# Attention with a routed FFN on one core: where ScalarE copies the transposed inverse sums out of PSUM

## The reference

```python
s1 = jnp.einsum('bhtd,bhsd->bhts', q1, k1) * scale + mask
s2 = jnp.einsum('bhtd,bhsd->bhts', q2, k2) * scale + mask
a1 = jax.nn.softmax(s1, axis=-1)
a2 = jax.nn.softmax(s2, axis=-1)
diff = a1 - lam * a2
out = jnp.einsum('bhts,bhsd->bhtd', diff, v)
```

## Time and profile before

| | |
|---|---|
| runs, device time | 2269.70, 2272.86, 2258.52 us (median 2269.7) |
| the profiled execution | 2265.93 us, span of the core 2264.1 us |
| TensorE busy | 1808.6 us (80% of the span) |
| VectorE busy | 1458.3 us (64%) |
| ScalarE busy | 1129.6 us (50%) |
| GpSimd busy | 614.6 us (27%) |
| granted TensorE clock, mean | 0.878 of full speed |
| attention | about 58 to 1520 us of the span |
| L763, the copy that is moved | 128 instructions |

### The profile page before, as it was taken

One profiled execution on the slowest core, in us unless ns is written; L12 is line 12 of the kernel. 1 busy time (PEld: TensorE's weight loads), 2 busy tenths in 40 slices (PEclk: granted clock), 3 DMA queues, 4 the chain that ended last, 5 costly groups with the idle time before them and its releaser, 6 DMA issues. The chain is left out here.

```text
span 2264.1 us, 37174 instructions
## 1 busy us (share of the span) xinstructions
PE 1808.6 (80%) x9826; PEld 1336.3 (59%) x9827; DVE 1458.3 (64%) x3278; ACT 1129.6 (50%) x3263; POOL 614.6 (27%) x504
## 2 busy tenths in 40 slices
PE   3678898898889879879888888967099999999700
PEld 3455555656655755655655564544099999999600
DVE  2588867878788788787787878751333333333366
ACT  1466756667566575676667766661122222222133
POOL 2222312412231242241232223110542222200165
PEclk7788898899889889799989989988599999999855
DMA  7855534545454463453545455320543333223288
GB/s 262 282 139 152 145 99 140 178 112 149 134 166 120 126 200 114 124 174 103 159 151 147 129 152 168 75 75 19 181 146 112 112 114 120 74 83 98 73 269 269
DMA packets 142837, 319.51 MB, mean 141 GB/s; under 512 B 16704, under 2 KB 19264, under 8 KB 140512
## 3 DMA queue, kind: packets, MB, share of 16 engines
q1 hardware_dynamic: 113280, 241.84, 37.8%
q0 software_dynamic: 14432, 48.64, 6.4%
q10 hardware_dynamic: 14976, 27.27, 3.2%
HBM read 215.97 MB, written 109.05 MB: 144 GB/s over the span
## 5 line engine op out<-in xcount | busy, mean ns | idle before, releaser
L735 ACT ACTIVATE expd<-S,neg_max 128x128 f32<-128x128 f32 (+3 forms) x1024 | 530.7, 534 | 158.7 <-DVE neg_max L878 156.2
L878 DVE TENSOR_REDUCE neg_max<-S 128x2 f32<-128x768 f32 (+3 forms) x384 | 399.7, 1041 | 278.9 <-PE S L598 277.5
L909 DVE SCALAR_TENSOR_TENSOR mixed<-expd,rho 128x384 f32<-128x384 f32 (+3 forms) x512 | 337.2, 678 | 0.3 <-issue 0.3
L747 ACT ACTIVATE probsT<-PTp 128x512 f32<-128x512 f32 (+2 forms) x384 | 203.7, 531 | 254.0 <-PE PTp L609 251.3
L490 POOL TENSOR_TENSOR swapped<-swapped,rope_t 128x512 f32<-128x512 f32 x80 | 103.3, 1291 | 767.2 <-DVE swapped L864 767.2
L594 PE MATMUL S<-kT,qT 128*128 128x256 f32 (+2 forms) x1024 | 285.8, 382 | 27.4 <-DMA qT<-parts_rows 13.4
L609 PE MATMUL PTp<-ident,mixed 128*128 128x128 f32 x1280 | 221.3, 290 | 102.3 <-DVE mixed L909 99.7
L644 PE MATMUL tail<-wo,ctxT 128*128 128x512 f32 x512 | 252.9, 622 | 24.9 <-ACT ctxT L779 22.2
L594 PEld LDWEIGHTS S<-kT,qT 128*128 128x128 f32 x1024 | 165.7, 199 | 127.5 <-issue 82.4
L1311 ACT ACTIVATE xT_hi<-xTp 128x512 fp32r<-128x512 f32 x72 | 43.1, 599 | 359.2 <-DVE yo L1487 348.9
L609 PEld LDWEIGHTS PTp<-ident,mixed 128*128 128x128 f32 x1280 | 145.3, 148 | 126.6 <-DVE mixed L909 123.5
(11 more groups left out here) (206 smaller groups left out, 3631.1 us busy)
## 6 DMA issues: line engine op xcount, KB each, us to landing
qT<-parts_rows SPq DMA_DIRECT2D x256, 256.0 KB, 4.6
parts_rows<-parts SPq DMA_DIRECT2D x160, 256.0 KB, 2.0
wqk<-wqk_split SPq DMA_DIRECT2D x75, 512.0 KB, 5.2
xin<-expert_in_rows SPq DMA_DIRECT2D x72, 256.0 KB, 2.9
expert_out_rows<-yo ACTq DMA_DIRECT2D x72, 256.0 KB, 3.2
kT<-parts_rows SPq DMA_DIRECT2D x64, 256.0 KB, 4.3
x<-in_x SPq DMA_DIRECT2D x8, 1024.0 KB, 7.8
x_rows<-x SPq DMA_DIRECT2D x8, 1024.0 KB, 7.0
```

The source lines that it names most:

```text
L735: ex = nc.scalar.activation(expd[s % 3][:, k * slot:k * slot + w], S[s % 2][:, k * slot:k * slot + w], ACT.Exp, bias=neg_max[s % 3][:, k:k ...
L747: nc.scalar.activation(probsT[i % 2][:, 0:i + 1, half:half + n, pair, :].rearrange("p j a q -> p a j q"), PTp[:, 0:w].rearrange("p (a j q) ...
L878: nc.vector.tensor_reduce(neg_max[s % 3][:, 0:k], v, AX, ALU.max, negate=True).then_inc(max_ready, 1)
L909: ins = nc.vector.scalar_tensor_tensor(out=mixed[sl % 3][:, a * 256:a * 256 + w], in0=e2, scalar=rr[:, i, h:h + 1], in1=e1, op0=ALU.mult, ...
```

## The change

In ScalarE's walk through the steps, the call of `take_scale` stands behind `exps` instead of in front of `take_probsT`. The condition is the same, so each of the 128 copies stays in its step. The short code behind the last batch (`end`), which has two of the copies, is as it was.

```diff
             def body(b, par, first, last):
                 for s, kv, u in steps(b, first, last):
-                    if (s - LAG_V - 1) % NU in LAST_OF and lagged(b, s, LAG_V + 1, first):
-                        take_scale(tile_no(b, s, LAG_V + 1))
                     if lagged(b, s, LAG_T, first):
                         take_probsT(*lagged(b, s, LAG_T, first), tile_no(b, s, LAG_T))
                     exps(s, u)
+                    if (s - LAG_V - 1) % NU in LAST_OF and lagged(b, s, LAG_V + 1, first):
+                        take_scale(tile_no(b, s, LAG_V + 1))
                     if (s - 2) % NU in LAST_OF and lagged(b, s, 2, first):
                         widen(*lagged(b, s, 2, first), tile_no(b, s, 2))
```

## The result

The changed kernel takes 2284.6 us (median of 12 runs, 2278.4 to 2292.2) against 2269.6 us (12 runs, 2258.5 to 2272.9). The ratio is 1.007, with a 95% interval of 1.0053 to 1.0088: slower by 12 to 20 us. Forecast were +33 us and 2302. The direction is right, the time is inside the stated range, and the size is off by a factor of two. The time is just under the forecast's own 2285 to 2320 and inside the 2270 to 2290 of the first rival. The profiled execution has a span of 2280.0 us (before 2264.1), and all of the difference but about 3 us lies between the first maximum of attention and the last.

A forecast was written before the change was run, and what follows sets the result against it. Each batch was taken as bound by a loop between engines, chiefly TensorE and VectorE. Removal 0 plus mean 4.1 us added per batch made 33 us over eight; from median 2270 that gave 2303, stated 2302, range 2268 to 2338.

The forecast's parts named there:

- the first rival: "The waits are absorbed": slack at the 16 places and TensorE catching up leave half or less, 2270 to 2290 us; chance 0.28.
- What goes away: Copy no longer in front of `probsT` on ScalarE: charged at nothing, since ScalarE would wait for the same transposes; bound 49 us.
- What is added: VectorE's L917 waits for the later copy, delaying the next maximum: 6.3 us in one batch, 5.2 in the next, 46 over eight.
- three kinds of places: Of 16 per batch: seven where VectorE is late itself, four where the maximum waits for scores, five where new waits count.
- (a): Step 8 of the second kv head: maximum 1.3 us later, 0.8 us after slack.
- (b): Step 0: maximum 1.8 us later, 0.7 in the next batch; after slack 1.4 and 0.3 us.
- (d): Step 8 of the fourth kv head: maximum 1.2 us later, no slack taken off.
- (e): Step 12 of the batch: maximum 1.2 us later but covered by ScalarE's `ctxT` work; only the copy counts, 0.4 us.
- (c): Step 4: maximum 0.8 us later, no slack taken off.
- How much reaches the end: Share of VectorE's new waits that delays TensorE: 4.7 us in one batch, 3.6 in the next, 33 us over eight.
- Faster: ScalarE no longer idles in front of the copy, 0.384 us gained per copy on the path, down to 2217 us; chance 0.06.
- The clock rival: Added waits lower TensorE's granted clock from 0.89 to 0.86 in a batch, 45 us in all, 2344 us; chance 0.08.

The follow-up runs named there:

- e4: Kernel before with only the copies of step 6 (tile 0) moved behind the exponentials: ratio 1.001, +2 us.
- e11: Changed kernel with VectorE's product (L917) of tiles 1 and 2 behind the maximum of steps 9 and 1: 2270.2 us, ratio 1.0023 to the kernel before.
- e1: Kernel before with only the 32 copies of step 8 (tile 1) moved behind the exponentials: ratio 1.0043, +9.7 us.
- e2: Kernel before with only the copies of step 0 (tile 2) moved behind the exponentials: ratio 0.9966, -7.7 us.
- e3: Kernel before with only the copies of step 4 (tile 3) moved behind the exponentials: ratio 1.0027, +6.1 us.
- e5: Kernel before with only the 8 copies in step 12 of a batch moved behind the exponentials: ratio 0.9965, -7.9 us.
- e6: Kernel before with all copies moved behind the exponentials except those in step 12 of a batch: ratio 1.0093, +21 us.
- e9: e1 with VectorE's product (L917) of tile 1 behind the maximum of step 9: ratio 1.0027 to the kernel before, +6 us.
- e10: Kernel before with only VectorE's order changed, product of tile 1 behind the maximum of step 9: ratio 1.0044, +10 us.
- e12: Kernel before with two extra unused products filling TensorE's wait ahead of the output projection: ratio 0.9919, -18 us, median 2248.4 us.

## Why the prediction was half right

**What goes away: nothing. Right.** `probsT` waits 93 us more, the copy 92 us less; e4 shows no gain.

**What is added, the waits at L917. Right in kind.** All three kinds of places are there: no wait in the 32 copies of step 6, new waits elsewhere that the next wait for scores takes back, and 1.0 to 1.2 us at (a), (b), (d) and (e), 0.6 at (c). What each was worth, as the change of the distance from maximum to maximum (start of L878 to start of the next), averaged over the six middle batches of the profiled executions, in us per batch:

| place, steps of the batch | forecast | changed kernel | alone | e11, maximum first except at (c) |
|---|---|---|---|---|
| (a) steps 20 to 22 | 0.8 | +0.69 | +0.69 (e1) | -0.02 |
| (b) steps 0 and 1 | 1.4 and 0.3 | +0.45 | +0.13 (e2) | +0.09 |
| (c) steps 4 to 6 | 0.8 | +0.64 | +0.64 (e3) | +0.64 |
| (d) steps 44 to 47 | 1.2 | +0.62 | +0.77 (e1) | -0.05 |
| (e) steps 12 and 13 | 0.4, for all of (e) | +0.75 | +0.75 (e5) | +0.17 |
| behind (e), step 16 | in the 0.4 | -1.84 | -2.04 (e5) | -1.90 |

The last column shows the cause: with the maximum ahead of the product, (a) and (d) are gone, and (c), where the order is as it was, is unchanged.

**How much reaches the end. Wrong at (e).** The step that failed reads: "There the later maximum is covered; what isn't covered is the copy itself [...]: 0.4 us." The first half holds. Counted from the maximum of step 12, the four instructions of L644 start at 14.87 us in the kernel before and at 15.13 in the changed kernel and in e5 (in six of the seven batches each, within 0.01): 0.26 us later, since the copy delays ScalarE's work on `ctxT`, and the 0.75 us of steps 12 and 13 only shorten TensorE's wait. What failed is the silent term behind that wait: that the work there takes as long as before. TensorE's four instructions in the earlier trace rows are granted 2.4 GHz instead of 1.2, and the maximum of step 17 comes at 19.0 us instead of 20.4. So (e) as a whole, steps 12 to 16, is worth -1.4 us per batch in e5, and -1.0 in the changed kernel, where one of the six batches has the slow rate and +1.3. That row stood ahead of the prediction with its 3.39 us; the 1.90 us of wait was read off it and the duration was not. Four steps later the same quarter of the next tile takes 1.88 us in the same trace:

```profile
682.22 1.88 PE L644 MATMUL tail<-wo,ctxT 128*128 128x512 f32 x4
```

With -1.0 instead of +0.4 per batch the sum of 33 us falls by 11 us. The isolated runs agree: the prediction's sum without (e) is 30 us, e6 measured 21 (13 to 29); e5 measured -8 (-3 to -13) where (e) had +3.

**The rest of the error is (b) and (d)**: 0.85 on the mean taken for 0.45, and 1.2 for 0.6, another 8 us. At (d) no slack was taken off on the ground that exponentials follow the maximum at once. They did, but the next maximum came 1.0 us later and about half of that was regained in the two steps behind, as at (a) (1.16 and 0.5). Only (c) regained nothing. The delays themselves came out 0.1 to 0.2 us shorter than the prediction's, since the copy starts 0.11 us before the last instruction of the exponentials ends and its reader starts within 0.05 us of its end. At (b) even 0.45 is too much: in four of the six batches step 0 is 0.55 us longer and step 1 is 0.48 shorter. The mean comes from two batches in which step 0 is 1.3 and 1.6 us longer, and in the same two batches of e1, where that copy stands in front, it is longer by 1.5 and 1.4.

**Rivals.** The measured 2284.6 us lies in the range of "The waits are absorbed", and partly for its reason: slack took about half a microsecond at (a), (b) and (d). It is not an explanation of the total, since e3 costs the 6 us forecast for it and e1 10 of the 16 forecast for (a) and (d), while the largest single term is the gain behind (e). "Faster" did not happen; e4 and e9 against e10 leave no room for more than a few microseconds. The clock rival was the right mechanism with the wrong sign: it was priced only as a loss from added waits. It was also read from a mean over 49 us, where the one place that mattered was 3.4 us long. And its two rows don't show what it read from them: TensorE is busy for 88% of the time in the earlier trace rows and for 89% in the earlier trace rows, so the lower clock of the second is not a matter of more idle time.

**What stays open.** Which idle time costs TensorE its full rate here. It is 1.9 to 2.0 us and slow in seven of seven batches of e1, e3 and, six times, of the kernel before; 1.5 to 1.8 us and quick in seven of seven of e2 and e5; but 2.0 to 2.2 us and quick in four batches of e6 and most of e11, and 3 us and slow in single batches of several kernels. The length of the wait ahead of the products doesn't decide alone. What TensorE did before that wait differs between these kernels, and I have not separated it. That e12 fills the wait and gets the rate shows that the idle time is needed for the loss, not how much of it. Nor is it shown why the later copy of step 12 brings the rate back; e5 shows that it does, in seven of seven batches.

The rate also moves at places that no edit touches, and the totals contain that. Step 39 of a batch takes 10.1 us at a granted clock of 0.66 or 8.5 us at 0.80, with the same instructions. Of the six middle batches one is quick in the kernel before and in the changed one, none in e3, all six in e1, four in e12. In e1 that is 1.3 us per batch against the 1.5 us that (a) and (d) add there, so its +9.7 us is not the price of its waits alone. Step 33 goes the other way: it is longer than in the kernel before by 0.1 to 1.4 us in every other kernel, the fastest included.

Open is also why the order on VectorE costs 10 us in e10. Its profiled execution has steps 16 and 33 longer by 0.6 and 0.8 us, which are not the edited ones; at step 16 that is two batches that reach the wait early, and step 15 is shorter by as much.

## What to carry to other kernels

Before a copy is moved back on its engine, look up its reader and what is queued behind that reader: here a 0.4 us copy in a place where its engine was idle anyway held up the next maximum on another engine. Look for slack at every such place: of five, three regained about half a microsecond, one regained nothing, and one was covered by another engine's work. And wherever an engine's rate can change, read the duration of the work behind a wait beside the length of the wait: four instructions at 3.4 us that take 1.9 elsewhere cost nearly as much as the wait that the waits view shows, and two useless products in the gap brought 0.8%, the best version found here (2248 us), where four, which overran it, brought 0.3%.

## What the hardware showed that was not expected

- The cost of an idle stretch of TensorE of 1.9 us was the stretch and another 1.2 to 1.7 us behind it, at a granted clock of about 0.54 to 0.6 in the kernel before and 0.54 to 0.57 in e1 for the next four instructions (PEclk of e1 at that place, third figure from the end):

```profile
657.60:661.10 3.50, 3.49 (x5) 1.64 (x6) 0.42 (x1) 1.55 (x6) 0.00 (x0) 0.55 1.03 217
```

- The total of a stage can hide it: over the seven stretches of about a batch (176 to 188 us) from 240 us on, the granted clock was 0.88 to 0.94 in the changed kernel and 0.89 to 0.92 in the one before, with no order by which the faster one could be told.
- Per step, the profiled executions repeat from batch to batch and from kernel to kernel within some 0.03 us at most steps that an edit doesn't reach. The exceptions are steps 3, 8, 15, 33 to 36, 39, 41, 43 and 47, where it is a tenth of a microsecond to 3 us; those whose granted clock was looked at (15, 33, 39) were quick at the higher one and slow at the lower. Away from them the difference of single steps shows a tenth of a microsecond, where the totals needed nine to twelve runs each for 4 us.
